# Mirrored order of node tiles when the front half meets more buckets, five look-ups a step instead of eight, and two products with zeros in every step of the edge pass

## What the kernel computes

```python
h = jnp.concatenate([x[row], edge_attr], axis=1)          # row = src
h = jax.nn.relu(h @ W1a + b1a) @ W1b + b1b
sums = jax.ops.segment_sum(h, col, num_segments=n_nodes)  # col = dst
counts = jax.ops.segment_sum(jnp.ones((h.shape[0],)), col, num_segments=n_nodes)
agg = sums / jnp.clip(counts, 1.0)[:, None]
z = jnp.concatenate([x, agg, u[batch]], axis=1)
return jax.nn.relu(z @ W2a + b2a) @ W2b + b2b
```

## Time and profile before

| what | us |
|---|---|
| median of 3 runs (8996.03 to 9005.73) | 8997.42 |
| the profiled execution, its own time | 9031.9 |
| the span of its profile | 9030.2 |

### The profile page before, as it was taken

How to read it: one execution, slowest core, us unless ns; L and a number is a source line. 1 busy time by engine, 2 the same in 40 slices (tenths; PEclk the granted TensorE clock), 3 DMA queues, 4 the chain that set the end, 5 groups by cost and what they waited for, 6 DMA issues and landing times. The chain is left out here.

```text
span 9030.2 us, 137943 instructions
## 1 busy us (share of the span) xinstructions
PE 6296.6 (70%) x36507; PEld 4249.3 (47%) x36507; DVE 6360.5 (70%) x17765; ACT 2836.5 (31%) x6169; POOL 2691.6 (30%) x2966
## 2 busy tenths in 40 slices
PE   4767777777555666566501788599997777777779
PEld 3545555555312222222201777444445666666668
DVE  6777777777668999655588999611024777777778
ACT  0222222222245776344400788300001333320000
POOL 0666767766646200000000000000002444444430
PEclk9666666666667999799855999799999999999999
DMA  2333333333498555699597666276676776752256
GB/s 98 94 96 95 97 97 97 96 97 97 127 393 270 163 169 145 227 337 329 163 387 311 207 215 213 95 245 217 215 251 178 180 183 179 181 144 63 63 105 194
DMA packets 1048196, 1605.78 MB, mean 178 GB/s; under 512 B 111567, under 2 KB 699236, under 8 KB 1033906
## 3 DMA queue, kind: packets, MB, share of 16 engines
q1 hardware_dynamic: 761756, 1179.89, 41.4%
q0 software_dynamic: 111328, 277.62, 9.5%
q10 hardware_dynamic: 174394, 139.51, 5.8%
HBM read 1177.49 MB, written 419.08 MB: 177 GB/s over the span
## 5 line engine op out<-in xcount | busy, mean ns | idle before, releaser
L774 POOL DMA_INDIRECT bucketed<-arena,wide x1563 | 1527.1, 977 | 882.6 <-issue 850.6
L2161 PE MATMUL psum<-wide,arena 128*128 x6496 | 1210.4, 329 | 397.5 <-DVE arena L2220 391.5
L2161 PEld LDWEIGHTS psum<-wide,arena 128*128 128x128 f32 x6496 | 989.2, 195 | 616.9 <-issue 491.8
L2220 DVE TENSOR_SCALAR arena<-wide,tile_first 128x128 f32 x3248 | 871.4, 302 | 469.4 <-PE psum L2161 289.8
L2082 POOL DMA_INDIRECT arena<-table,src_i x832 | 802.0, 964 | 1006.9 <-PE psum L2178 870.8
L942 PE MATMUL psum<-arena 128*128 128x512 bf16 x2304 | 705.8, 444 | 425.5 <-DVE arena L890 247.4
L662 PE MATMUL psum<-w_edge,arena 128*128 128x256 f32 x1568 | 869.7, 655 | 0.0
L890 DVE TENSOR_SCALAR arena<-sums 128x512 bf16<-128x512 int16 x2304 | 821.1, 356 | 0.0
L691 ACT CAST wide<-psum 49x49 f16<-49x49 f32 x1568 | 310.8, 198 | 1556.0 <-PE psum L669 893.9
L2030 POOL DMA_DIRECT2D table<-wide x13 | 9.6, 736 | 2478.5 <-DVE wide L1929 2478.5
L1686 PE MATMUL psum<-sums,arena 128*128 128x129 f32 x4802 | 602.3, 281 | 154.3 <-DVE arena L1676 154.3
(11 more groups left out here) (475 smaller groups left out, 12384.7 us busy)
## 6 DMA issues: line engine op xcount, KB each, us to landing
arena<-halved SPq DMA_DIRECT2D x441, 384.0 KB
arena<-adjacency SPq DMA_DIRECT2D x98, 1568.0 KB, 7.8
adjacency<-wide SPq DMA_DIRECT2D x588, 256.0 KB, 2.3
arena<-adjacency SPq DMA_DIRECT2D x196, 640.0 KB, 3.9
arena<-adjacency SPq DMA_DIRECT2D x147, 768.0 KB, 6.8
arena<-bucketed POOLq DMA_DIRECT2D x208, 528.0 KB, 6.1
halved<-arena SPq DMA_DIRECT2D x147, 384.0 KB, 6.3
wide<-bucketed ACTq DMA_DIRECT2D x208, 256.0 KB
```

The lines of the kernel that those rows point to most:

```text
L774: e.indirect_dma_start(bucketed, bass.IndirectOffsetOnAxis(ap=places[k][0:size, c:c + 1], axis=0), rows[k][0:size, c, :], None).then_inc(s ...
L2161: e.matmul(flat[:, ds((chunk & 3) * 512 + 2048, P)], lhsT=hot[:, i % 8, :], rhs=table_in[:, ds(tile * P, P)], start=False, stop=True, skip ...
L2220: e.tensor_scalar(hot[:, i % 8, :], rows[:, ds((chunk[k] & 15) * P, P)], tile_first[:, ds(tile[k], 1)], None, op0=ALU.is_equal).then_inc(l ...
```

## The change

Five things, all from one idea on the order of the dst tiles:

1. `which_half` counts from `hist`, before the positions are made, how many look-ups there are in all and how many fall in chunks 0 to 831. If the near half has more than half, `turn_round` is 1: the dst tiles are placed in mirrored order (a product of `hist` with the mirroring matrix `swap`), and the first pair used is `lead` = 832 less the pairs in use. The steps run in the same chain as `positions`.
2. With at most half of the look-ups in the near half, LOOKS becomes 2080, and `PER_PAIR` 5: all 416 steps have five.
3. Two products with zeros (`keep_awake`, 128 x 384) stand before each far product.
4. For a mirrored order: zeros are written to the first 112 chunks too (`fill_spare`), `fill_last` waits for both writes, block b of chunks is searched up to b + 1 (`chunk_blocks`, so `turn(1)` stands ahead of `find(0)`, and each of the 18 blocks of hits but the last ones has one more pick), and SP reads the column of each stored tile from `tile_column` into a register, four at a time.
5. Chunks without look-ups ahead of the first one get an end of 1, and `s_looked` begins at 1.

```diff
-LOOKS = -(-(NEAR + BUCKETS_49 + 2) // 16) * 16
+MOST_LOOKS = (2 * (N_EDGES // (PAIR * P) + TILES) + BUCKETS_49 - TILES) // 2 + TILES
+LOOKS = -(-(MOST_LOOKS + 2) // 80) * 80
-PER_PAIR = 8
+PER_PAIR = 5
+LEAD = -(-2 * (PAIRS - N_EDGES // (PAIR * P)) // 16) * 16
...
+            e.dma_start(bucketed_v[:, 0:LEAD, :].rearrange("p (r c) w -> p r (c w)", c=16),
...
-                e.wait_ge(s_empty, 16)
+                e.wait_ge(s_empty, 32)
...
+        which_half = [
...
+            ("tensor", lambda e, _: e.matmul(psum[0:TILES, 2, 0:1], lhsT=ones[0:TILES, 0:TILES], rhs=n_pairs, start=True, stop=True), 1),
...
+            ("vector", lambda e, _: e.tensor_scalar(lead, psum[0:TILES, 2, 0:1], -1.0, float(PAIRS), op0=ALU.mult, op1=ALU.add), 1),
...
+            ("vector", lambda e, _: e.scalar_tensor_tensor(turn_round, both_sums[:, 1:2], 2.0, both_sums[:, 0:1], ALU.mult, ALU.is_gt), 1),
+            ("vector", lambda e, _: e.tensor_tensor(lead, lead, turn_round, ALU.mult), 1),
...
+            ("tensor", lambda e, _: e.matmul(psum[0:TILES, 1, 0:TILES], lhsT=swap, rhs=hist, start=True, stop=True), 1),
+            ("vector", lambda e, _: e.tensor_copy(hist, psum[0:TILES, 1, 0:TILES]), 1),
+        ]
...
-                return [m for m in range(b - LAG, b + 1) if 0 <= m < CHUNK_BLOCKS]
+                return [m for m in range(b - LAG, b + 2) if 0 <= m < CHUNK_BLOCKS]
...
                     turn(0)
+                    turn(1)
                     find(0)
...
-                            turn(b + 1)
+                            turn(b + 2)
...
+                    e.sem_inc(s_looked, 1)
...
+                        for _ in range(2):
+                            keep_awake(e, psum[:, n % 4, P:512], n < 4)
                         for c in range(PAIR):
...
-                                e.wait_ge(s_clear, chunk[k + 1])
-                                if i >= 8:
-                                    e.wait_ge(s_looked, i - 6)
+                                e.wait_ge(s_clear, chunk[min(k + 1, PER_PAIR - 1)])
+                                if i >= 7:
+                                    e.wait_ge(s_looked, i - 5)
```

More of the change, by code:

```diff
@@ L413, in fill_last @@
             return emit
-        positions = [
+        first_i, final_i, next_i = (spread49[k].bitcast(i32) for k in (1, 2, 3))
+        filled, looks, looks_in, looks_at, flag, more_in = (spread49[k] for k in (4, 5, 6, 7, 8, 9))
+        swap = spread49[10]
+        both_looks, both_sums = spread49[11][:, 0:2], spread49[11][:, 2:4]
+        turn_round, lead, mirror, row_to, column_by, column_from = (spread49[12][:, k:k + 1] for k in range(6))
+        tile_column = sb("tile_column", [1, TILES], i32)
+        which_half = [
             ("vector", hist_wait, 1),
@@ new lines, in build @@
+            ("vector", lambda e, _: e.tensor_tensor_scan(incl, ones[0:TILES, 0:TILES], hist, 0.0, ALU.mult, ALU.add), 1),
+            ("vector", lambda e, _: e.tensor_scalar(ends, incl, pair_at256, None, op0=ALU.add), 1),
+            ("vector", lambda e, _: e.tensor_tensor(first_i, ends, hist, ALU.subtract), 1),
+            ("vector", lambda e, _: e.tensor_scalar(final_i, ends, -1.0, None, op0=ALU.add), 1),
+            ("vector", lambda e, _: e.tensor_single_scalar(first_i, first_i, 7, op=ALU.arith_shift_right), 1),
@@ new lines, in build @@
+            ("vector", lambda e, _: e.tensor_single_scalar(final_i, final_i, 7, op=ALU.arith_shift_right), 1),
+            ("vector", lambda e, _: e.tensor_single_scalar(filled, hist, 0.0, op=ALU.is_gt), 1),
+            ("vector", lambda e, _: e.scalar_tensor_tensor(looks, final_i, 1.0, first_i, ALU.add, ALU.subtract), 1),
+            ("vector", lambda e, _: e.tensor_tensor(looks, looks, filled, ALU.mult), 1),
+            ("vector", lambda e, _: e.tensor_reduce(both_looks[:, 0:1], looks, axis=AX.X, op=ALU.add), 1),
@@ new lines, in build @@
+            ("vector", lambda e, _: e.tensor_scalar(looks_at, final_i, float(NEAR - 1), 1.0, op0=ALU.min, op1=ALU.add), 1),
+            ("vector", lambda e, _: e.tensor_tensor(looks_at, looks_at, first_i, ALU.subtract), 1),
+            ("vector", lambda e, _: e.scalar_tensor_tensor(looks_at, looks_at, 0.0, filled, ALU.max, ALU.mult), 1),
+            ("vector", lambda e, _: e.tensor_reduce(both_looks[:, 1:2], looks_at, axis=AX.X, op=ALU.add), 1),
+            ("tensor", lambda e, _: e.matmul(psum[0:TILES, 1, 0:2], lhsT=ones[0:TILES, 0:TILES], rhs=both_looks, start=True, stop=True), 1),
@@ new lines, in build @@
+            ("vector", lambda e, _: e.tensor_single_scalar(tile_column[:, :], tile_column[:, :], 7, op=ALU.arith_shift_left), 1),
+            ("tensor", lambda e, _: e.matmul(psum[0:TILES, 1, 0:TILES], lhsT=swap, rhs=hist, start=True, stop=True), 1),
+            ("vector", lambda e, _: e.tensor_copy(hist, psum[0:TILES, 1, 0:TILES]), 1),
+        ]
+        positions = which_half + [
+            ("vector", lambda e, _: e.tensor_reduce(tot, hist, axis=AX.X, op=ALU.add), 1),
+            ("vector", lambda e, _: e.tensor_scalar(tot_i, tot, float(PAIR * P - 1), None, op0=ALU.add), 1),
+            ("vector", lambda e, _: e.tensor_single_scalar(tot_i, tot_i, 8, op=ALU.arith_shift_right), 1),
+            ("vector", lambda e, _: e.tensor_copy(n_pairs, tot_i), 1),
+            ("tensor", lambda e, _: e.matmul(psum[0:TILES, 1, 0:1], lhsT=before[0:TILES, 0:TILES], rhs=n_pairs, start=True, stop=True), 1),
+            ("vector", lambda e, _: e.tensor_scalar(pair_at, psum[0:TILES, 1, 0:1], lead, None, op0=ALU.add), 1),
@@ L439, in build @@
             ("vector", lambda e, _: e.memset(t_all, 0.0), 1),
[L440 to L441 removed]
+            ("vector", lambda e, _: e.tensor_copy(looks, high_i), 1),
+            ("tensor", lambda e, _: e.matmul(psum[0:TILES, 1, 0:TILES], lhsT=swap, rhs=looks, start=True, stop=True), 1),
+            ("vector", lambda e, _: e.tensor_copy(t_sb[0][0][0:TILES, :], psum[0:TILES, 1, 0:TILES]), 1),
+            ("vector", lambda e, _: e.tensor_copy(t_sb[0][1][0:TILES, :], psum[0:TILES, 1, 0:TILES]), 1),
+            ("tensor", lambda e, _: e.matmul(psum[0:TILES, 1, 0:TILES], lhsT=swap, rhs=low, start=True, stop=True), 1),
+            ("vector", lambda e, _: e.tensor_copy(low, psum[0:TILES, 1, 0:TILES]), 1),
             ("vector", lambda e, _: e.memset(units, 1.0), 1),
@@ L814, in build_adjacency @@
             head = part(h, 0, 3 * CHUNKS).rearrange("p (w c) -> p w c", w=3)
-            picks = [part(wide2, 2 * HITS + 64 * m, 64).bitcast(bf16) for m in range(LAG + 1)]
+            picks = [part(wide2, 2 * HITS + 64 * m, 64).bitcast(bf16) for m in range(LAG + 2)]
             from_one = part(sums, 0, 256).bitcast(i16)
@@ L868, in turn_and_pick @@
                     def turn_and_pick(b):
-                        if b < CHUNK_BLOCKS:
-                            e.wait_ge(s_turn, b + 1)
-                            e.tensor_copy(turned[:, b, :, :].rearrange("p w n -> p (w n)"), psum[:, 4, 0:3 * P]).then_inc(s_turned, 1)
+                        for m in ([0, 1] if b == 0 else [b + 1]):
+                            if m < CHUNK_BLOCKS:
+                                e.wait_ge(s_turn, m + 1)
+                                e.tensor_copy(turned[:, m, :, :].rearrange("p w n -> p (w n)"), psum[:, 4, 0:3 * P]).then_inc(s_turned, 1)
                         if b:
@@ L980, in store_blocks @@
                     def store_blocks(i, rows):
+                        _, column = nc.values_load_multi_w_load_instructions(
+                            tile_column[:, i * BANKS:i * BANKS + rows], engines=(ENG.SP,), min_val=0, max_val=(TILES - 1) * P,
+                            skip_runtime_bounds_check_because="first node of a tile, made by this program from the tile's number")
                         for b in range(rows * GROUPS):
```

33 lines of the change are left out of this document (21 added, 12 removed).

## The result

The changed kernel takes 9094.19 us (median of 4 runs, 9089.29 to 9102.61) where the kernel before takes 8997.77 us beside it: a ratio of 1.0106, 95% interval [1.0089, 1.0124]. It is slower by 96 us, 1.1%. The prediction said 8513 us; the result lies 414 us above the upper end of its range, 8680, on the side that had a chance of 0.03. The profiled execution took 9102.61 us, with a span of 9100.9.

The account below looks back on a forecast made before the run. TensorE's sequencer, with VectorE close behind, was taken to bound the edge pass. Stage 45 + 381 x 3.0 + 35 x 2.85 = 1288 us, −510, other edits +26: 9031.9 to 8548 profiled, 8513 by the median; range 8430 to 8680.

Parts of the forecast that it names:

- register loads: In each edge-pass step, on TensorE and VectorE: loading five values takes 0.38 us, saving 0.42 us a step.
- The stage: Edge pass, from just ahead of the first eviction to the last far product: 1288 us for 1798, −510 us.
- TensorE's term: TensorE's floor in an edge-pass step: 1.62 + 1.57 − 0.42 = 2.77 us, giving steps of 3.0 us.
- VectorE's chain: VectorE's time in an edge-pass step: 2.68 us plus 0.08 for tile numbers, 2.76 us.
- the lower clock: Edge pass, rival: TensorE granted 1.2 GHz throughout, steps of 3.8 to 4.95 us, 9330 us at 4.95; chance 0.03.
- Products with zeros: TensorE in each edge-pass step: hidden, costing nothing; the rival, not hidden, 0.35 to 0.42 us a step, chance 0.10.
- The order: Edge pass: tiles placed mirrored, 1906 near look-ups, 25 pairs left empty, first look-up 45 us later.
- wasted entries: Look-up list of the edge pass: 174 wasted entries for 1226, where nearly all of the gain lies.
- `which_half`: Ahead of `last_i`: 31 steps of VectorE and 4 of TensorE add 9 us, with nothing running beside them.
- `turn(1)` and the picks: Adjacency stage: second turn 25 us after the first, costing about 12 us; 18 more picks cost 4 us.
- The 26 us ahead of the edge pass: Chain to `last_i`, extra turn, picks and side work: 9, 12, 4 and 1 us, together +26 us.

Follow-up runs that it names:

- shifted lists: Kernel before with both look-up lists one entry further in SBUF, so loads of eight start off a multiple of four: 10809.91 us for 9707.72.
- aligned loads: Changed kernel with both engines loading eight entries from a multiple of four and using five: 9391.28 us for 9707.72, ratio 0.9708.
- table of loads: Kernel before with 108 extra register loads on VectorE ahead of the edge pass, 1 to 8 and 16 values at offsets 0 to 3: 9458.83 us.
- two half edits: Changed kernel with aligned loads of eight on TensorE's queue alone, then on VectorE's alone: 9087.76 and 9090.22 us for 9009.74, both ratio 1.0091.
- shorter list: Kernel before with a list of 2080 entries in place of 3248, still eight look-ups a step: 8814.46 us for 9028.36, ratio 0.977.

## Why the prediction was wrong

- **The step that failed** is the one headed "register loads": "I take 0.38, a line between the two rows", with "bounds are 0.31 and 0.59". They measure 1.17 us on TensorE and 1.06 to 1.14 on VectorE in the mean, 1.08 and 1.04 by the four medians. The line went through rows of four and eight values that all started at a multiple of four; that the new loads start at 5n stood in the diff, and no row of before shows a load that starts elsewhere. The bounds were no bounds. The shifted lists, the aligned loads and the table of loads show it; that it goes through both engines is shown by the two half edits.
- **The size of the miss.** By the profiled executions it is 9102.6 for the forecast 8548, 555 us. The stage took 572 us more than forecast (1860 for 1288), the parts ahead of it and behind it some 17 less. The term explains the stage: 2 x (1.08 - 0.38) x 416 = 582 us. The other 26 us of the miss by the medians, 581, are the profiled execution's distance from the median, put at 34.5 and measured at 8.4.
- **The rest of TensorE's term was right.** A floor of 2.77 us plus 0.24 gave 3.0. With loads of four to eight aligned values the step is 3.00 us on a chip like that of the record, without the zeros and the mirrored order, and 3.2 on a slower one with or without them. What costs the 0.2 us there was not settled.
- **VectorE's chain** was put at 2.76 with 0.76 of loads in it. With the 2.26 that its unaligned loads take it is 4.26, and where it sets the step, with TensorE's loads aligned, the step is 4.33. That term was right too but for the loads.
- **The only case that ended slower**, the lower clock with 0.03, did not come true, although the clock fell to 0.83 and 0.81. The step is 4.35 to 4.41 us at clocks of 0.75, 0.76 and 0.83, and 3.35 at 1.00 once the loads alone are shorter.
- **Products with zeros**: hidden, as forecast; the clock, forecast at 0.95 or more, was 0.83 and 0.81, as both engines waited longer. With short loads it is 0.97 with no zeros at all.
- **The order**: mirrored, as the counts said; lead 39 us for 45. It brings nothing: with aligned loads and the order kept the time is the same. That the wasted entries and not the mirroring hold the gain is shown by the shorter list, with 0.977 alone and 0.940 with five aligned look-ups a step, both without mirroring.
- **`which_half`**: 9 us were forecast at `last_i` and 23.0 came, 14.5 of them SP's stall behind the second write of zeros and the other 8.5 near the forecast. The scatters absorb most of it: 7.9 us are left at the last scatter.
- **`turn(1)` and the picks**: the second turn came 25.9 us after the first (25 forecast). From POOL's first copy to the last store of `adjacency` the stage takes 1206.6 us for 1186.7, 19.9 longer for the 16 forecast; the eight other kernels with these edits have 1200 to 1208, those without them 1178 to 1189.
- **The 26 us ahead of the edge pass** were therefore right: 7.9 + 19.9 = 28. That the first gather is only 12 us late comes from the stages between, which no edit touches: from the last store to the first gather the changed kernel took 3271 us for 3287, and over all the kernels but that of the table on VectorE this stretch lies between 3261 and 3287.

## What to carry to other kernels

Load registers from lists in groups of four that start at a multiple of four entries (counted in the tile, as the list moved by one entry shows: its loads of eight began at 8n of the list and took 1.94 us), and pad or carry values over where the number per step is not such a multiple: five unaligned values (1.18 us) cost more than sixteen aligned ones (1.11). Before a duration is interpolated between rows, list what the rows have in common (here the alignment) and ask whether the new case shares it. Where two engines' chains are nearly equal, an edit to one shows almost nothing (0.06 us a step here, and 1.04 for both); both have to be changed to see whether either matters.

## What was not expected of the hardware

- A register load off a multiple of four entries takes 0.31 us for one value and 0.22 for each more, 1.18 for five and 3.60 for sixteen, against 0.62 and 1.11 from such a multiple. TensorE does the same (1.24 for five, 1.94 for eight, 0.59 for eight aligned). ACT's loads of four take 0.31; it had no others here.
- Issuing a small DMA held SP's queue for 13.40 us behind two large writes of zeros. In the kernel before, with one such write ahead, the two small ones took 0.56 and 1.15 us.
- On two of the chips every kernel's stage of scatters took 2800 to 2900 us for 2178, with ACT waiting 294 to 331 us in 1000 for a releaser that the trace calls remote. Nothing here shows what it is.
